# Attention products of four successive units issued in one run, with eight probability buffers

## The reference

```python
o1 = _attn(q, k1, v1, causal)            # branch 0: all earlier tokens, 1024 keys
o2 = _attn(q, ks, vs)                    # branch 1: 256 selected tokens
o3 = _attn(q, kw, vw, winmask)           # branch 2: causal, the last 64 tokens
o = g[:, 0] * o1 + g[:, 1] * o2 + g[:, 2] * o3
return o.transpose(0, 2, 1, 3).reshape(B, T, N_HEAD * VDIM) @ Wproj
```

## Time and profile before

| | us |
|---|---|
| median of 3 runs (2938.94 to 2940.89) | 2940.07 |
| the profiled execution | 2938.53 |
| its span in the trace | 2936.4 |

### The profile page before, as it was taken

The page is one execution under the profiler, slowest core; times in us unless marked ns, Lnnn a source line. Parts: engine busy times, 40 slices in busy tenths (PEclk is TensorE's granted clock), DMA queues, the critical chain, the costliest instruction groups (busy, mean ns, idle before and its releaser), DMA issues. The chain is left out here.

```text
span 2936.4 us, 47406 instructions
## 1 busy us (share of the span) xinstructions
PE 2361.4 (80%) x16660; PEld 1563.1 (53%) x16660; DVE 1690.2 (58%) x3159; ACT 1219.0 (42%) x2665; POOL 536.5 (18%) x575
## 2 busy tenths in 40 slices
PE   5666766665499999799999799999899999630896
PEld 3444535443365666465666465666465665320785
DVE  4754847466455664555665555665555665450676
ACT  2323423233054554354554355455355455410442
POOL 0230504215000110100110100110100110136332
PEclk9777877877699999899999899999899999855997
DMA  2361715427846556446556446556546643241113
GB/s 91 139 243 36 288 58 211 170 89 293 183 102 131 122 125 128 106 102 136 122 119 126 106 104 137 127 109 126 115 104 131 132 104 73 91 84 48 48 51 109
DMA packets 222999, 361.11 MB, mean 123 GB/s; under 512 B 68810, under 2 KB 124717, under 8 KB 222384
## 3 DMA queue, kind: packets, MB, share of 16 engines
q1 hardware_dynamic: 218448, 349.72, 47.7%
q0 software_dynamic: 4320, 8.43, 0.9%
HBM read 230.10 MB, written 126.56 MB: 121 GB/s over the span
## 5 line engine op out<-in xcount | busy, mean ns | idle before, releaser
L1342 ACT ACTIVATE prob<-ps 128x512 f32<-128x512 f32 (+5 forms) x1600 | 637.5, 441 | 740.8 <-PE ps L1293 587.5
L1395 DVE TENSOR_REDUCE maxima<-ps 128x1 f32<-128x512 f32 (+3 forms) x768 | 387.1, 547 | 299.2 <-PE ps L1224 151.2
L1314 PE MATMUL ps<-prob,plain 128*32 128x512 f32 (+5 forms) x3200 | 512.1, 443 | 0.0
L1400 DVE TENSOR_REDUCE maxima<-ps 128x2 f32<-128x512 f32 (+1 forms) x512 | 294.5, 607 | 245.0 <-PE ps L1232 98.6
L1365 POOL TENSOR_TENSOR products<-products,sums 128x256 f32<-128x256 f32 x192 | 140.7, 733 | 1611.3 <-DVE sums L1386 1610.1
L1386 DVE RECIPROCAL sums<-sums 128x256 f32<-128x256 f32 x192 | 331.5, 1736 | 104.2 <-ACT sums L1353 104.2
L1285 PE MATMUL ps<-q1a_s,k1a_s 128*128 128x512 f32 (+3 forms) x768 | 303.1, 395 | 0.0
L1293 PE MATMUL ps<-q1b_s,k1b_s 128*128 128x512 f32 (+3 forms) x768 | 301.1, 393 | 0.0
L1314 PE MATMUL ps<-prob,v_s 128*32 128x512 f32 (+3 forms) x1536 | 284.3, 491 | 0.0
L1221 PE MATMUL ps<-k1a_s,q1a_s 128*128 128x512 f32 (+3 forms) x768 | 233.3, 372 | 8.7 <-DMA k1a_s<-k1ah_dram 8.3
L1285 PEld LDWEIGHTS ps<-q1a_s,k1a_s 128*128 128x128 f32 x768 | 147.1, 192 | 126.8 <-issue 118.1
(11 more groups left out here) (329 smaller groups left out, 4774.3 us busy)
## 6 DMA issues: line engine op xcount, KB each, us to landing
qh_dram<-pairs SPq DMA_DIRECT2D x96, 512.0 KB, 3.7
kwh_dram<-pairs SPq DMA_DIRECT2D x64, 512.0 KB, 2.7
qa_s<-qh_dram SPq DMA_DIRECT2D x128, 256.0 KB, 4.5
kwa_s<-kwh_dram SPq DMA_DIRECT2D x128, 256.0 KB, 7.6
q1a_s<-qh_dram SPq DMA_DIRECT2D x128, 256.0 KB, 4.7
qb_s<-qh_dram SPq DMA_DIRECT2D x64, 256.0 KB, 9.2
kwb_s<-kwh_dram SPq DMA_DIRECT2D x64, 256.0 KB, 10.0
k1a_s<-k1ah_dram SPq DMA_DIRECT2D x32, 512.0 KB, 6.8
```

Source lines behind the costliest of these rows:

```text
L1314: mm = pe.matmul(ps[at:at + VD, SCORES + k % 2, q0 - c * CH:q0 - c * CH + w], w_, m.prob[:, n % PROBS, h, 0:w], start=first, stop=True, sk ...
L1342: act.activation(m.prob[:, u % PROBS, h, 0:w], ps[:, turn % SCORES, 0:w], ACT.Exp, scale=SCALE).then_inc(s["exp_done"], 1)
L1395: ins = dve.tensor_reduce(partial[:, h, i, part:part + 1], bank[:, 0:w], AX, ALU.max)
L1400: ins = dve.tensor_reduce(negs[1 if kind == "max1" else 2][:, at:at + 2], bank.rearrange("p (i n) -> p i n", i=2)[:, :, 0:w], AX, ALU.max, ...
```

## The change

The products of four successive units are issued in one run, after the scores of the unit behind them, where it was two. The last run of a side takes five. The probabilities get eight buffers instead of four.

```diff
-PROBS = 4
+PROBS = 8
+TOGETHER = 4
@@ def exact_pass(w):
     for u in range(len(UNITS) + 1):
         if u < len(UNITS):
             todo.append(("scores", w, u))
-        ready = range(u - 2, u) if u >= 2 and u % 2 == 0 else range(u - 1, u) if u == len(UNITS) else ()
+        ready = range(u - TOGETHER, u) if u >= TOGETHER and u % TOGETHER == 0 else ()
+        if u == len(UNITS):
+            ready = range(u - u % TOGETHER, u)
         for done in ready:
             todo.append(("products", w, done))
         for done in ready:
```

## The result

| | before | after |
|---|---|---|
| median of the runs, us | 2939.51 (4 runs, 2938.40 to 2940.89) | 3054.38 (4 runs, 3050.11 to 3056.74) |
| ratio to before | | 1.0389, 95% interval 1.0371 to 1.0407 |
| the profiled execution: its time, its span, us | 2938.53, 2936.4 | 3053.28, 3051.2 |
| PE busy, us and share of the span | (above) | 2364.0, 77% |

The kernel became 115 us slower. Slower was forecast, but by 67 us: 3054 lies outside the range of 2955 to 3045, and where rival (4), "the clock falls too" (3025 to 3065), had put it. That rival had a chance of 0.10.

A forecast was written before the change was run, and what follows sets the result against it. PE was taken to set the pace. Odd sides +48, even sides +21 and the remaining sides -1 gave +68 us on 2938.53, that is 3006.5, stated as 3007 us, range 2955 to 3045.

The forecast's parts named there:

- rival (4): PE's clock also falls after the new waits, giving 3025 to 3065 us; chance 0.10.
- Switches and ACT's waits: Between scores and products: half as many runs save 67 us, and PE's waits for an exponential's bank going saves 13.
- Odd sides: Every second pass over the 25 units: DVE's later reciprocals delay PE, net +3.2 us each, +48 us over 15.
- Even sides: The other passes: POOL's multiply uncovered after S2 adds 2.0 us; late rows add 1.9; +21 us over eleven.
- proj(1): Projection after S2 in even sides, no longer behind P0 and P1: its wait for POOL grows from 0.91 to 2.9 us.
- Rows: Row transfer behind a later local load delays the next side's S0: +1.9 us in each of eleven even sides.
- S19 waits about 1.0: Fills of unit 19's scores in odd sides wait about 1.0 us for banks whose reduces stand behind unit 12's second reciprocal.
- proj(0): Projection late in odd sides: waits 2.0 us for the last reciprocal and POOL's multiply, of which 0.3 was there.
- the clock: Half-rate stretches after PE's new waits of about 2 to 2.9 us: 18 to 57 us more, left out of the sum.
- fills max1(0,3): Spare-bank use after S7 in odd sides: PE waits 2.4 us in all for DVE to return this and the next bank.
- (2): Switches only: DVE's three banks cover the longer runs, PE gains 80 us, 2859 us; chance 0.08.
- (3): Waits are about half of those walked, as DVE catches up earlier and rows land earliest: 2957 us; chance 0.12.

The follow-up runs named there:

- the last two kernels: Changed kernel with rows ahead of the local load, projections and divides behind product runs: runs of four 2847.15 us, the same order with runs of two 2920.63 us.
- the third experiment: Changed kernel with each projection put behind the next run of products: 2968.40 us, ratio 1.0101.
- the pair with short reciprocals: Each reciprocal cut to one column of 256, leaving out work: in the changed kernel 2865.58 us, in the kernel before 2898.99 us.
- rows and projections together: Changed kernel with row transfers before the local load and projections behind product runs, reciprocals still between fills: 2952.97 us, ratio 1.0044.

## Why the prediction was wrong

Right were the direction, the mechanism of each wait, and their sizes.

- **Switches and ACT's waits** (80 us): 73.5 measured between the last two kernels. If 13 of these are ACT's, a switch saved was worth (73.5 - 13) / (32 x 6) = 0.32 us instead of 0.35. The lists of the two kernels show only 6 us for ACT (22.5 and 16.5); with those a switch is worth 0.35. The Trainium skill, "TensorEngine Tiling (Array Packing)", section "Key Properties", says that changing the tiling mode drains TensorE, and gives no price. That pair of runs agrees that such a change costs time, and gives a price.
- **Odd sides** (+3.2): an undisturbed odd side lasts 58.06 and the forecast is 58.05 with the row before it. At each of its four places walk and trace differ by 0.12 at most.
- **Even sides** (+2.0 for proj(1)): 0.91 became 2.76; the undisturbed side is 0.25 longer than forecast.
- **Rows** (+1.9, 11 times, 21 us): 15 times, 20.8 us in all. Side 0 of each block has them as well, which I had put at about nothing, and each is somewhat shorter. The sum held, the split did not.
- **"S19 waits about 1.0"**: right here, but I did not see that proj(0)'s wait covers half of it. It shows as soon as proj(0) is moved, in the third experiment and in that of rows and projections together.

**The step that failed is the clock.** The prediction's section on it said that the new waits "come near to what made it fall", priced the falls at 18 to 57 us from the rows, and then put them at nothing in the sum and gave them a chance of 0.10. What the runs showed in its place: 34 falls, and 48 of the 115 us from the clock. The price of one was nearly right, 1.5 us where 1.6 to 1.7 were measured. Its count of waits was not: besides the 12 it has 26 of about 2 us, but its own walk gives 15 fills max1(0,3), 15 proj(0) and 11 rows, which is 41, so one place is missing, and that 34 falls came out near the 38 counted is in part luck. The chance was wrong. The only evidence against falls was that waits up to 0.9 us stay at clock 1.00, and that says nothing on waits of 2 to 2.9. The evidence for them was nearer than the prediction read it. In the first of the two windows of the earlier trace rows PE is busy for 0.44 us, and stops at 1218.44; a mean of 0.95 with two levels is 0.3 us at half clock, so the clock fell at about 1220.7, 2.3 us after PE had stopped. The walked wait of 2.9 us is longer than that. A term between 0 and 57, whose nearest row on the one side is 0.9 us and on the other 2.3, belongs into the sum with a value between, not into a rival. With half of it (28) the forecast would have been 3035.

The Trainium skill, "TensorE: Matmul & The Clock Gate", section "Why this matters for your kernels", tells one to leave no idle gaps above about 3 us between bursts of matmuls. By that rule the waits here, none above 2.9, would all have been safe; the trace disagrees: 32 of the 42 waits of 1.8 to 2.8 us at these three places were followed by half clock. The measurement decides.

Rivals (2), switches only, and (3), half the waits, are out: all waits are there at full size.

What stays open: a few us in the pair with short reciprocals and in rows and projections together, why moving the rows ahead brought more half clock, and why 10 of 42 such waits brought no fall. No row here shows what decides between these and the 32, nor why a wait of 1.7 to 2.1 us for a row brings a fall less often (4 of 12 over all traces) than one of 1.8 for the fill (52 of 75).

## What to carry to other kernels

Before making runs of one engine's work longer, list what stood between them: each was cover for a wait of somebody else, and an operation that was ready in time behind two units is late behind none. Then sum PE's new waits one by one, and where one is near 2 us or more, add the half clock that follows it (1.6 us each here) to the sum and not to the risks. The gain of the longer runs was real all the time (73 of 80 us forecast), and moving the projections, the divides and the rows to places where they are covered turned a loss of 115 us into a gain of 93.

## What the runs showed of the hardware

- One wait of PE of 1.8 to 2.8 us in an otherwise busy stretch can be enough for the granted clock to go from 1.00 to 0.50, during the wait or within 2.3 us behind it. Over all traces, inside blocks: waits of 2.8 us in 34 of 36 cases, of 2.0 in 22 of 30, of 1.8 for the fill in 52 of 75, of 1.7 to 2.1 for a row in 4 of 12, and waits up to 1.6 us never. A fall is shown for 3.4 us, some for 6.8 (14 in four of the kernels), and one of 3.4 cost 1.6 to 1.7 us.
- Idle time cost more than useless work: 17 or 26 added small matmuls ahead of each of the 32 projections made the kernel 44 us faster.
- A change between 128-column and 32-column tiles and back costs 0.32 to 0.35 us and counts as busy time: two kernels with PE busy at 99.3% and 98.7% in the same 100 us differ by 73.5 us.
